# Spreading the router's combine weights through DRAM, merged loads, and early work dealt out anew, in an attention and mixture-of-experts kernel

## The reference, cut to what matters

```python
x = x + L0_xattn(layernorm(x), ctx, ctx, mask, ...)      # energy = QK^T/sqrt(8) + rpe_table[bucket]
x = x + L0_ffn(layernorm(x), U1, V1, b1, U2, V2, b2)     # gelu(x @ U1 @ V1 + b1) @ U2 @ V2 + b2
x = x + L1_xattn(layernorm(x), ctx, ctx, ...)
x = x + L1_ffn(layernorm(x), ...)
# L1_ffn, on xf = all tokens:
logits = l2norm(xf) @ l2norm(gate_w).T
topk_scores, topk_idx = top_k(sigmoid(logits), 8)
combine = one_hot(topk_idx) weighted by topk_scores / sum(topk_scores)       # tokens x 16
y = einsum("neh,ehd->ned", silu(xf @ w_gate) * (xf @ w_up), w_down)
out = einsum("ned,ne->nd", y, combine) + silu(xf @ sw_gate) * (xf @ sw_up) @ sw_down
```

## Time and profile before

| | |
|---|---|
| median of 3 runs (range) | 346.16 us (345.96 to 347.55) |
| the profiled execution | 346.3 us, of which its span is 343.8 us |
| TensorE matmul, busy | 182.1 us (53%), 1875 instructions |
| VectorE, ScalarE, GpSimd, busy | 112.8, 106.7, 95.0 us |
| granted TensorE clock, mean | 0.772 of full |
| DMA | 17.96 MB in 33078 packets |

### The profile page before, as it was taken

How to read it: one execution, slowest core, us unless ns; L and a number is a source line. 1 busy time by engine, 2 the same in 40 slices (tenths; PEclk the granted TensorE clock), 3 DMA queues, 4 the chain that set the end, 5 groups by cost and what they waited for, 6 DMA issues and landing times.

```text
span 343.8 us, 4955 instructions
## 1 busy us (share of the span) xinstructions
PE 182.1 (53%) x1875; PEld 124.8 (36%) x1875; DVE 112.8 (33%) x273; ACT 106.7 (31%) x189; POOL 95.0 (28%) x179
## 2 busy tenths in 40 slices
PE   2059189849995989700089600099699200460006
PEld 1045034436652556600078500077478100450006
DVE  5224755318558457600004300037655200010000
ACT  1016556726551758600036300034543100010000
POOL 5508531014652143000295000342153000500014
PEclk9999589969995699965559965569899755585557
DMA  5796632223022112877501877511003877277760
GB/s 153 238 183 133 127 79 56 50 61 86 20 51 57 26 45 55 29 42 35 19 0 8 33 36 33 60 38 47 11 2 11 33 35 34 11 27 36 39 36 15
DMA packets 33078, 17.96 MB, mean 52 GB/s; under 512 B 12032, under 2 KB 32352, under 8 KB 33056
## 3 DMA queue, kind: packets, MB, share of 16 engines
q1 hardware_dynamic: 33056, 17.66, 46.6%
HBM read 5.04 MB, written 0.55 MB: 16 GB/s over the span
## 4 chain that ended last, share of the span: by engine, by line
PE 30%; SPq 24%; issue 22%; DMA 11%; POOL 5%; DVE 5%; ACT 2%; POOLq 0%
SPq L270 14%; PE two_s L1151 5%; DMA cbS<-combT 5%; SPq L248 5%; PE two_s L1143 4%; PE one_m L1285 4%; SPq L206 4%; PE two_s L1258 3%; PE one_m L1197 2%; DMA stack_Q<-nmT 2%; POOL hid_h L469 2%; PE one_m L1229 2%; PE one_m L1093 2%; POOL xn L424 2%; PE one_m L1119 2%
## 5 line engine op out<-in xcount | busy, mean ns | idle before, releaser
L469 POOL TENSOR_TENSOR hid_h<-hid_h,cbS 128x512 f32<-128x512 f32 x16 | 20.0, 1268 | 133.3 <-DMA cbS<-combT 133.3
L882 DVE TENSOR_REDUCE mx<-two_s 128x8 f32<-128x1024 f32 x32 | 38.1, 1220 | 50.3 <-PE two_s L1151 49.9
L1285 PE MATMUL one_m<-wd,hid_h 128*128 128x128 f32 x128 | 21.5, 332 | 57.0 <-POOL hid_h L469 57.0
L1285 PEld LDWEIGHTS one_m<-wd,hid_h 128*128 128x128 f32 x128 | 20.0, 242 | 58.5 <-POOL hid_h L469 57.3
L602 ACT ACTIVATE pt_p<-two_s 128x1024 f32<-128x1024 f32 x32 | 32.0, 1024 | 24.7 <-PE two_s L1151 24.5
L1093 PE MATMUL one_m<-ident,xn 128*128 128x128 f32 x32 | 7.4, 318 | 59.2 <-POOL xn L424 58.7
L550 ACT ACTIVATE xnT<-one_m 128x256 f32<-128x256 f32 x16 | 6.1, 383 | 70.7 <-PE one_m L1093 70.7
L1093 PEld LDWEIGHTS one_m<-ident,xn 128*128 128x128 f32 x32 | 3.8, 154 | 62.2 <-POOL xn L424 60.2
L424 POOL TENSOR_SCALAR xn<-xr,mv,rstd 128x128 f32<-128x128 f32 x32 | 25.9, 817 | 1.7
L939 DVE TENSOR_TENSOR hid_h<-hid_h,two_s 128x512 f32<-128x512 f32 x16 | 10.9, 683 | 39.2 <-ACT hid_h L640 33.9
L1197 PE MATMUL one_m<-pt_p,va 128*32 128x128 f32 x512 | 21.5, 296 | 0.2 <-ACT pt_p L602 0.2
(11 more groups left out here) (116 smaller groups left out, 325.2 us busy)
## 6 DMA issues: line engine op xcount, KB each, us to landing
cbS<-combT SPq DMA_DIRECT2D x64, 64.0 KB, 7.9
stack_K<-ksp SPq DMA_DIRECT2D x48, 64.0 KB, 2.1
stack_Q<-qsp SPq DMA_DIRECT2D x48, 64.0 KB, 2.1
cbS<-rel_bias_scratch SPq DMA_DIRECT2D x3, 224.0 KB, 4.1
wg<-in_wg SPq DMA_DIRECT2D x1, 544.0 KB, 4.0
wu<-in_wu SPq DMA_DIRECT2D x1, 544.0 KB, 4.8
xr<-in_x SPq DMA_DIRECT2D x4, 128.0 KB, 3.4
cx<-in_ctx SPq DMA_DIRECT2D x4, 128.0 KB, 2.8
```

What stands on the lines that cost most here:

```text
L469: pool.tensor_tensor(h[:].rearrange("p (c t) -> p c t", c=2), h[:].rearrange("p (c t) -> p c t", c=2), cbS[:, p % 2, 2 * u:2 * u + 2], ALU ...
L882: free(dve.tensor_reduce(mx[:, l, p % 2, b, c].rearrange("p a j -> p (a j)"), src[:].rearrange("p a (j k) -> p (a j) k", j=4), AX.X, ALU.m ...
L1285: ins = pe.matmul(dst[:, b * D:(b + 1) * D], h[:, at_col:at_col + SEQ], wd[:, 2 * u + k], start=False, stop=(n == UNITS), skip_group_check ...
```

## The change

1. **Combine weights.** `store_weights(p)` writes the 16x256 tile to a DRAM scratch by one DMA; `spread_weights(p)` waits for it and reads it back by two DMAs of 64 partitions, instead of 16 DMAs from SBUF.
2. **Loads.** 30 loads on SP become 10, of which two (expert weights) stand between `max_rows(0, 1, 0)` and `max_rows(0, 1, 1)`; two more loads (`first`, `wqk`) are issued by ScalarE. The mask comes from the host as 16 repeated bf16 copies by two DMAs that GpSimd issues; `mask_bf16` and `spread_masks` are gone.
3. **Copies and clears.** The eight window copies go four to VectorE, two to ScalarE, two to GpSimd, two of the first four for the scores on VectorE; four of the eight stack clears go to GpSimd.
4. **Norms.** GpSimd keeps the power (and -mean times it, `shift_of`); the two tiles are written by VectorE before attention 0 and by ScalarE elsewhere.
5. **Order.** All lists and the slot table are written anew to go with it.

In the cut below `load_masks`, `power` and `shift_of` are GpSimd's, `normalize(n, p)` and the two `act.dma_start` ScalarE's; `minus` is taken in VectorE's `variance`; the last piece is the end of TensorE's list.

```diff
-CLEARED = ("Q00", "K00", "Q10", "K10", "Q01", "K01", "Q11", "K11")
+CLEARED = ("K00", "Q00", "K10", "Q10", "K01", "Q01", "K11", "Q11")
+NORM_ON = ('DVE', 'ACT', 'ACT', 'ACT')
...
+    comb_d = nc.dram_tensor("combine_scratch", (2, EXPERTS, TOK), F32, kind="Internal").ap()
...
+            def store_weights(p):
+                freed(sp, f"ct{p}")
+                sp.dma_start(comb_d[p % 2], combT[:, p % 2]).then_inc(sem("comb_stored"), 16)
+
             def spread_weights(p):
-                freed(sp, f"ct{p}")
+                sp.wait_ge(sem("comb_stored"), 16 * (p + 1))
                 if p >= 2:
                     sp.wait_ge(sem("weighted"), UNITS * (p - 1))
-                for e in range(EXPERTS):
-                    r = 64 * (e % 2)
-                    src = combT[e:e + 1, p % 2].unsqueeze(1).broadcast_to([1, 64, TOK])
-                    sp.dma_start(cbS[r:r + 64, p % 2, e // 2], src).then_inc(sem(f"spread{p % 2}_in"), 16)
+                for k in range(2):
+                    src = bass.AP(tensor=comb_d.tensor, offset=(p % 2) * EXPERTS * TOK + k * TOK,
+                                  ap=[[0, 64], [2 * TOK, ECH], [1, TOK]])
+                    sp.dma_start(cbS[64 * k:64 * k + 64, p % 2], src).then_inc(sem(f"spread{p % 2}_in"), 16)
...
+            load(rel_in, rel_in_d, "rel")
+            load_x(1, 4)
+            load_ctx(0, 1)
+            load_ctx(1, 4)
+            load_x(0, 1)
             load(rowb[:], rows_d.partition_broadcast(128), "rows")
...
             fixed_rows(0, 0)
             fixed_rows(1, 0)
-            spread_masks()
+            load(second[:], second_d, "second")
+            load(small, small_d, "small")
             store_windows()
-            stack("K", 0, 1, 0)
+            fixed_rows(0, 1)
             stack("K", 0, 0, 0)
+            stack("K", 1, 0, 0)
             load_windows()
...
             max_rows(0, 1, 0)
-            stack("Q", 1, 0, 2)
+            load(wgu[:], wgu_d, "wgu")
+            load(wdown[:], wdown_d, "wdown")
+            max_rows(0, 1, 1)
             stack("K", 1, 0, 2)
...
+            store_weights(0)
             spread_weights(0)
-            spread_weights(1)
             stack("Q", 0, 1, 2)
             stack("Q", 1, 1, 2)
+            store_weights(1)
             stack("Q", 2, 1, 2)
+            spread_weights(1)
...
+            store_weights(2)
             spread_weights(2)
+            store_weights(3)
             spread_weights(3)
...
+            def load_masks():
+                for t in range(2):
+                    pool.dma_start(bias["ST"[t]][96:128], masks_d[t].rearrange("r (g h k) -> r g h k", g=4, h=HEADS))\
+                        .then_inc(sem("masks_in"), 16)
...
+            def shift_of(n, p):
+                pool.wait_ge(sem(f"rstd{n}"), p + 1)
+                pool.tensor_tensor(shift[:, p], minus[:, p], rstd[:, p], ALU.mult).then_inc(sem(f"shift{n}"), 1)
...
             residual(2, 2)
-            normalize(2, 2)
+            power(2, 2)
+            shift_of(2, 2)
+            weigh(0, 0)
+            weigh(0, 1)
+            power(2, 3)
...
+            def normalize(n, p):
+                act.wait_ge(sem(f"shift{n}"), p + 1)
+                for b in range(2):
+                    ins = act.activation(xn[:, p, b], xr[:, p, b], ACT.Identity, bias=shift[:, p, b:b + 1],
+                                         scale=rstd[:, p, b:b + 1])
+                ins.then_inc(sem(f"norm{n}"), 1)
...
+            act.dma_start(first[:], first_d).then_inc(sem("first_in"), 16)
+            act.dma_start(wqk[:], wqk_d).then_inc(sem("wqk_in"), 16)
             bias_part(0)
...
+                if NORM_ON[n] == "ACT":
+                    dve.tensor_scalar(minus[:, p], mv[:, p, :, 0], -1.0, None, ALU.mult)
...
             gate_clamp()
-            variance(0, 3)
-            clear_stack("K01")
-            clear_stack("Q11")
-            clear_stack("K11")
-            window_s(0)
-            window_s(1)
-            window_s(2)
-            window_s(3)
+            normalize(0, 0)
+            normalize(0, 1)
+            normalize(0, 2)
+            normalize(0, 3)
             gate_scale()
+            value_bias()
+            window("S", 0)
+            second_ffn()
+            window("S", 1)
+            window("T", 0)
+            window("T", 1)
...
             turn_x(3, 2)
-            context(1, 3, 1, 1)
+            logits(2)
+            attention_out(1, 3)
             gate_up(2, 0)
-            attention_out(1, 3)
             gate_up(2, 1)
-            logits(2)
+            turn_weights(2)
             gate_up(2, 2)
+            gate_up(2, 3)
             turn_x(3, 3)
-            gate_up(2, 3)
-            turn_weights(2)
             gate_up(2, 4)
+            logits(3)
             gate_up(3, 0)
+            down(2, 4)
             gate_up(3, 1)
-            logits(3)
+            turn_weights(3)
             gate_up(3, 2)
-            down(2, 4)
             down(2, 0)
-            turn_weights(3)
+            gate_up(3, 3)
             down(2, 1)
-            gate_up(3, 3)
             gate_up(3, 4)
```

More of the change, by code:

```diff
@@ L350, in _ @@
+            stack("Q", 1, 0, 3)
             stack("Q", 0, 1, 0)
@@ L352, in _ @@
             stack("Q", 2, 1, 0)
+            max_rows(0, 2, 0)
+            max_rows(0, 2, 1)
+            max_rows(0, 3, 0)
             stack("Q", 0, 1, 1)
@@ L378, in _ @@
             stack("Q", 2, 1, 3)
+            max_rows(1, 2, 0)
             store(0)
-            max_rows(1, 2, 0)
-            store(1)
             max_rows(1, 2, 1)
@@ L755, in _ @@
[L755 removed]
             turned_max(1, 0, 0)
+            weights(0, 2, 0, 0)
+            weights(0, 2, 0, 1)
             turned_max(1, 0, 1)
@@ new lines, in _ @@
+            value_rows(0)
+            less_part("K", 1, 1, 0)
+            first_ffn()
+            value_rows(1)
+            turn_x(0, 0)
+            less_part("K", 0, 0, 1)
+            value_bias()
+            project("Q", 0, 0)
+            less_part("K", 1, 0, 1)
+            less_part("Q", 0, 0, 0)
+            turn_x(0, 1)
+            less_part("Q", 1, 0, 0)
+            second_ffn()
+            turn_gate()
+            project("K", 1, 1)
+            project("Q", 0, 1)
+            less_part("K", 0, 1, 1)
@@ L1373, in _ @@
-            turned(0, 0, 0, 0)
-            project("Q", 0, 2)
             scores(0, 1, 0, 1)
             project("Q", 0, 3)
+            scores(0, 1, 1, 0)
+            less_part("Q", 0, 0, 3)
             turn_max(0, 0, 1)
+            less_part("K", 1, 0, 2)
+            scores(0, 1, 1, 1)
+            less_part("Q", 1, 0, 3)
+            turn_max(0, 1, 0)
+            less_part("K", 0, 0, 3)
+            turned(0, 0, 0, 0)
+            value_rows(2)
+            turned(0, 0, 0, 1)
+            turn_max(0, 1, 1)
@@ L1423, in _ @@
             ffn_up(1, 0)
             ffn_up(1, 1)
+            scores(0, 2, 1, 0)
+            scores(0, 2, 1, 1)
+            turn_x(2, 0)
+            ffn_down(1, 0)
+            project("Q", 1, 0)
+            ffn_down(1, 1)
+            scores(0, 3, 0, 0)
+            scores(0, 3, 0, 1)
+            less_part("Q", 0, 1, 0)
+            turn_max(0, 2, 0)
+            less_part("Q", 1, 1, 0)
+            turn_max(0, 2, 1)
+            scores(0, 3, 1, 0)
+            scores(0, 3, 1, 1)
+            turn_x(2, 1)
@@ L1495, in _ @@
             attention_out(1, 1)
-            gate_up(0, 1)
+            turn_x(1, 2)
+            logits(0)
             context(0, 3, 1, 1)
-            gate_up(0, 2)
-            attention_out(0, 3)
             ffn_up(2, 0)
             ffn_up(2, 1)
+            gate_up(0, 0)
+            attention_out(0, 3)
+            ffn_down(2, 0)
+            gate_up(0, 1)
+            ffn_down(2, 1)
             turn_x(3, 1)
-            gate_up(0, 3)
-            ffn_down(2, 0)
+            turn_weights(0)
@@ L1537, in _ @@
+            turned(1, 2, 0, 0)
             down(1, 4)
             down(1, 0)
+            scores(1, 3, 1, 0)
             down(1, 1)
-            scores(1, 3, 0, 0)
-            turned(1, 2, 0, 0)
+            turn_max(1, 3, 0)
+            scores(1, 3, 1, 1)
+            context(1, 2, 0, 0)
+            turned(1, 2, 0, 1)
             down(1, 2)
-            turn_max(1, 2, 1)
+            turned(1, 2, 1, 0)
+            turned(1, 2, 1, 1)
+            context(1, 2, 0, 1)
+            turn_max(1, 3, 1)
@@ L1634 @@
     mask = a["mask_1x1xSxS2_bk1"].reshape(SEQ, SEQ)[:, ::-1]
+    on_heads = lambda m: _np.ascontiguousarray(
+        _np.broadcast_to(m.reshape(4, 32, 1, SEQ).transpose(1, 0, 2, 3), (32, 4, HEADS, SEQ))).reshape(32, -1).view(_np.uint8)
+    bits = lambda v: _np.ascontiguousarray(v).view(_np.uint32).view(_np.float32)
     consts, fixed = constants()
+    bqk = _np.stack([by_dim(a[f"L{l}_xattn_b{c}"].reshape(D)) for l in range(2) for c in "qk"], 1)
+    wo = [in_rows(a[f"L{l}_xattn_Wo"]) for l in range(2)]
```

(7 more changed lines are left out.)

809 lines of the change are left out of this document (376 added, 433 removed), and 37 rows, old and new, of the table SLOTS.

## The result

| | before | after |
|---|---|---|
| median (range) of 4 runs each | 346.24 us (345.96 to 347.55) | 208.10 us (205.52 to 209.03) |
| ratio, 95% interval | | 0.596 (0.590 to 0.602) |
| the profiled execution, its span | 346.3, 343.8 us | 208.6, 206.8 us |
| TensorE matmul, busy | 182.1 us (53%) | 173.4 us (84%) |
| granted TensorE clock, mean | 0.772 | 0.933 |

The kernel takes 40% less time. Medians and ranges in this document are of all executions, ratios of those within 1.5% of the kernel's fastest, since now and then an execution takes longer without any change in the kernel. The question of this study is therefore where the other 16 us came from.

What follows compares the result with a forecast made beforehand. It took the kernel to be bound mostly by TensorE, besides four all-idle stretches (103.3 us) behind the spreading DMAs. Sum: 343.8 - 25.3 - 24.1 - 54.5 - 15 - 4 - 1 + 2 = 221.9, plus 2.5: 224.4 us, range 211 to 246.

Steps and rivals of the forecast that it cites:

- X = 8: Combine-weight spread: its two loads from DRAM take 8 us, so 11.4 us from `combT` to landed weights, against 33.6.
- the end from `combT(2)`: Stretches 3 and 4, last two spreads: -52.9 + 0.4 us, with pair 3 landing right behind pair 2.
- the 20 given: Sign on GpSimd: its wait for the spread weights is under 20 us in all, not 133.
- the three signs named for a wrong forecast: First scores after 35, the end's two spreads over 12 us apart, or `max_rows(0, 1, 1)` landing over 10 us late.
- Stretch 1, -25.3: Pair 0's spread: the all-idle stretch goes entirely, 25.3 us, since TensorE has 21 us of other work.
- Stretch 2, -25.1 + 1: Pair 1's spread: the all-idle stretch of 25.1 us goes, except 1 us that stays.
- start: Before the first scores: earlier `ctx` load and fewer VectorE copies bring them near 27 instead of 41.88, -15 us.
- expert weights in the middle: 1664 KB loaded in front of `max_rows(0, 1, 1)` and pair 2's stacks: +2 us, up to 12 if cover is gone.
- norms: GpSimd's 24 norm tiles go to ScalarE at about 0.28 us each: -1 us, ends -4 and +7.
- clock: TensorE's matmuls at the lower clock after four dead stretches: -4 us, ends 0 and 8; granted clock above 0.85.
- `logits(2)`'s forecast -2: At the end, `logits(2)` runs right behind its input instead of 4 us later: half gained, 2 us.
- the steps are the same: At the start, from the `ctx` chain to the window loads nothing changes but an earlier begin, 13 us.

Runs made afterwards that it cites:

- b_spread: The kernel before with only the new spread (one store, two loads from DRAM), every list as it was: 248.89 us, ratio 0.713.
- a_oldspread: The changed kernel with the old spread of 16 DMAs a pair from SBUF put back and the store left out: 300.08 us, ratio 0.863.
- e_wgu_early: The changed kernel with the two expert-weight loads near the start of SP's list, ahead of the store of the windows: 206.38 us, ratio 0.600.
- a_poolnorm: The changed kernel with norm tiles of places 1 to 3 written by GpSimd again, not ScalarE: 211.12 us, ratio 0.602.
- b_spread_pool: The kernel before with the new spread, and on GpSimd four normalisations moved ahead of weighing: 237.71 us, ratio 0.682.
- c_clears: The changed kernel with GpSimd's two window copies given to VectorE and GpSimd's clears of three stacks moved ahead of `gate_power()`: 206.14 us, ratio 0.599.
- a_nopoolwin: The changed kernel with GpSimd's two window copies given to VectorE: 204.2 us, ratio 0.587.
- a_masklate: The changed kernel with GpSimd's two mask loads (1 MB) issued behind its last `power(0, p)`: 205.45 us, ratio 0.595.

## Why the prediction was right, and where it failed

**Right.** The bound (GpSimd's list standing behind the spreading DMAs), the part of the change that matters (100 of 137 us by b_spread alone), and the price of a spread's loads (X = 8, measured 7.6). Landings at the end are 9.2 us apart (8 forecast), the end from `combT(2)` is 28.3 us (29.2 forecast). Eight `cbS` issues; GpSimd's wait is 21.0 us, a little over the 20 given. First scores before 35, landings less than 12 apart, and `max_rows(0, 1, 1)`, the longest of its kind to land, in 5.6 us: none of the three signs named for a wrong forecast is there, and they would not have shown the step that failed.

**The step that failed** is "Stretch 1, -25.3" and "Stretch 2, -25.1 + 1". They were sized by the time in which *all* engines are idle. What TensorE lost is longer, 29.18 us until 173.50 and 28.76 us until 223.72 (the two rows under b_spread), since GpSimd's weighing, power and norm (3.7 us) came behind each landing and only then TensorE's input. These 7.5 us were never in the sum, and 1 us was left for a rest that did not stay: 8.5 of the 15.1 us by which the span's forecast (221.9) missed. The runs show it from both sides: the order alone is worth 11 us on the old kernel with the new spread, and undoing one step of it costs 10 to 12 us on the changed one. The forecast saw the norms leave their place behind `weigh(0, 0)`, but counted this as what makes the stretch vanish and not as a term of its own. It also read the new list wrongly in one point: not all five norms leave, `power(2, 3)` still stands behind `weigh(0, 0)`. With a spread of 9 us this costs nothing; with the old one TensorE waits 22.94 us for its norm (a_oldspread).

The sum, term by term, in spans:

| term | forecast | measured | from |
|---|---|---|---|
| stretches 1 and 2 | -49.4 | -57.9 | TensorE's two waits |
| the end, from `combT(2)` | -52.9 + 0.4 | -53.8 | 82.1 to 28.3 |
| start | -15 | -10.0, and 5.4 of TensorE's work brought ahead | 41.88 to 31.86 |
| expert weights in the middle | +2 | about 0 | TensorE's waits, e_wgu_early |
| norms | -1 | about -2.5, intervals overlap | a_poolnorm |
| clock | -4 | TensorE's busy time -8.7 | 182.1 to 173.4 |

The clock's row overlaps with the others (part of the 8.7 us lies in the two waits' neighbourhood), so these don't add up exactly; taking half of it on the path as the prediction did, they come to -57.9 - 53.8 - 15.4 + 0 - 2.5 - 4.35 = -134.0, and the span fell by 137.0. The rest, 3 us and `logits(2)`'s forecast -2 within it, is in the new order of the middle; it wasn't told apart further.

**Right in sum, wrong in its parts: the start.** Forecast -15, with first scores at 27. They came at 31.86. The prediction took "the steps are the same" and had no term for the masks' 1 MB and the other loads that now lie on the DMA engines together: `second`, on the chain that ended last, took 10.9 us to land (5.2 with the masks later), the store 9.7. Late masks brought the first scores to 29.77 and the whole nothing, so what sets 31.86 is shown only in part. But TensorE had by then done 21.2 us of work and not 15.8: of the 10 us gained and the 5.4 brought forward the term gets its 15. That the sum fits is luck.

**The clock** came out at 0.933, above the 0.85 given. b_spread has 0.881 with 180.8 us of TensorE's busy time, b_spread_pool 0.905 with 176.4, the changed kernel 0.933 with 173.4. The order of GpSimd's list alone thus took 4.4 us from TensorE's busy time, by one profile of each kernel: part of what it brought is clock. The term itself has a slip: its two rows, 5.28 and 5.78 us for two restarts, give 22 us for four and not 16, so 5.5 us and not 4.

## What to carry to other kernels

Size a stall by what the engine that bounds the kernel waits (the view of waits), not by the stretch in which all are idle: what stands in line between the landing and that engine's input belongs to it. A step that waits for a DMA should be as late in its engine's list as its users allow, even where the DMA takes only 9 us; on this kernel three steps too early cost 10 to 12 us. The rows that single partitions held and 64 had to read went faster through DRAM: 9.0 us with the store, in place of 33.6, for 1 MB. Both forms move it in pieces of 1 KB, but the change also made two DMAs of 16; whether the source or their number brought it wasn't tested.

## What the runs showed of the hardware that was not expected

**VectorE and GpSimd slow each other.** One window copy (96x2048 bf16) takes VectorE 0.68 us with GpSimd idle or at small work (24.23 above, and all six in c_clears); beside GpSimd's copies and clears it takes 3.51, 2.37 and 4.68 (28.14 and 31.57 above, the last two in one row), and GpSimd's own copy takes 1.88 us or 4.74. The Trainium skill, "SBUF — State Buffer", section "Who interferes with whom", says that such copies on VectorE can take a port pair that they share with GpSimd, and that the second to issue then blocks for the whole of the first. For the most part the trace agrees. Single rows of VectorE's last two copies and of GpSimd beside them:

```profile
31.57 2.37 DVE L886 COPY bias_t<-cbS 96x2048 bf16<-96x2048 bf16 x1
...
33.86 4.68 DVE L886 COPY bias_t<-cbS 96x2048 bf16<-96x2048 bf16 x1
...
36.20 1.80 POOL L387 MEMSET stack_Q<- 128x2048 bf16 x1
```

The first ends at 33.94, 0.54 us behind the end of GpSimd's copy (28.66 + 4.74 = 33.40); the second at 38.54, 0.54 us behind the end of GpSimd's last clear (38.00): each looks like a copy of 0.6 us that had to wait until GpSimd was through. In a_nopoolwin two copies end 1.16 us behind the second of two clears. The copy of 28.14 doesn't fit: it ends at 31.65, 2.96 us behind the end of GpSimd's first copy (28.69) and 1.75 before that of the second. Spans of GpSimd are rough in this profile, so this stays open.

**A small store behind large loads lands late.** 24 KB to DRAM took 9.7 us to land with the masks on the way and 3.4 us without them (the DMA views of the changed kernel and of a_masklate), and the 16 KB of combine weights 1.4 us later in the kernel. So a small transfer's time was here set by the large ones beside it. The issues of SP are slower then, too: five stack copies behind the store take 5.51 us of SP with the masks beside them, 3.16 without.
